# Arrays of a two-layer kernel placed at other byte addresses in SBUF

## The reference, cut to what matters

```python
nx = layer_norm(x); weights = softmax(nx @ Wq @ (ctx @ Wk).T / 16); evidence = weights @ (ctx @ Wv)
combined = concat([nx, evidence, cond])
h = silu(combined @ e_w1 + e_b1)              # 3 experts, 512 each
routed = sum((h @ e_w2 + e_b2) * softmax(combined @ router_W + router_b))
g = sigmoid(silu(combined @ gate_w1 + gate_b1) @ gate_w2 + gate_b2)
x = x + g * (routed @ out_w + out_b)
xq, xkv = ada_ln(x, cond), ada_ln(ctx, cond)
x = x + softmax(heads(xq @ Wq) @ heads(xkv @ Wk).T / 4) @ heads(xkv @ Wv) @ Wp
```

## Time and profile before

| | us |
|---|---|
| median of 3 runs (428.57, 431.21, 814.35) | 431.21 |
| the profiled execution | 429.68 |
| its span in the trace | 427.9 |
| TensorE busy with matmuls, of the span | 416.2 |
| VectorE busy | 327.5 |
| ScalarE busy | 225.6 |
| GpSimd busy | 171.2 |

### The profile page before, as it was taken

One profiled execution on the slowest core, in us unless ns is written; L12 is line 12 of the kernel. 1 busy time (PEld: TensorE's weight loads), 2 busy tenths in 40 slices (PEclk: granted clock), 3 DMA queues, 4 the chain that ended last, 5 costly groups with the idle time before them and its releaser, 6 DMA issues.

```text
span 427.9 us, 9498 instructions
## 1 busy us (share of the span) xinstructions
PE 416.2 (97%) x3541; PEld 382.9 (89%) x3541; DVE 327.5 (77%) x780; ACT 225.6 (53%) x495; POOL 171.2 (40%) x183
## 2 busy tenths in 40 slices
PE   6999989999999999999999999999999999999997
PEld 5787889899999889998999899989998998887866
DVE  1697686783876579859985799789849987994897
ACT  1887822516445644476348643862683358337272
POOL 1348484724622263225611725165315435332110
PEclk9999998999999999999999999999999999999999
DMA  8747440421300220032201300130003001410401
GB/s 293 233 157 276 173 147 2 92 57 45 70 1 5 63 64 6 23 100 51 72 7 51 75 1 2 55 75 2 3 14 88 2 4 32 106 26 2 100 2 49
DMA packets 16981, 28.06 MB, mean 66 GB/s; under 512 B 3816, under 2 KB 9128, under 8 KB 16936
## 3 DMA queue, kind: packets, MB, share of 16 engines
q1 hardware_dynamic: 16808, 27.45, 22.2%
q10 hardware_dynamic: 128, 0.01, 0.0%
HBM read 16.20 MB, written 2.10 MB: 43 GB/s over the span
## 4 chain that ended last, share of the span: by engine, by line
PE 87%; DVE 6%; ACT 4%; issue 2%; DMA 1%; DVEq 0%; ACTq 0%
PE hidden_banks L1658 9%; PE hidden_banks L1659 9%; PE hidden_banks L1660 9%; PE token_bank L1658 6%; PE token_bank L1659 6%; PE token_bank L1660 6%; PE score_banks L1665 5%; PE score_banks L2027 5%; PE score_banks L1997 4%; PE value_bank L2050 3%; PE hidden_banks L1878 3%; PE value_bank L2053 3%; PE value_bank L1665 3%; PE head_bank L1665 2%; PE value_bank L2061 1%
## 5 line engine op out<-in xcount | busy, mean ns | idle before, releaser
L1592 POOL TENSOR_TENSOR hidden_low<-hidden,hidden_high 128x512 fp32r<-128x512 f32 x56 | 72.9, 1302 | 139.3 <-ACT hidden_high L1023 139.2
L1015 ACT ACTIVATE hidden<-hidden_banks 128x512 f32<-128x512 f32 x56 | 33.3, 599 | 64.2 <-PE hidden_banks L1878 64.1
L1658 PE MATMUL hidden_banks<-normed_high,hidden_w_high 128*128 128x256 f32 x224 | 66.1, 295 | 0.8 <-DVE hidden L1348 0.8
L1431 DVE TENSOR_REDUCE head_maxima<-score_banks 128x2 f32<-128x308 f32 x128 | 56.5, 473 | 11.0 <-PE score_banks L1997 9.3
L1083 ACT ACTIVATE exp_ring<-score_banks 128x512 f32<-128x512 f32 x96 | 53.3, 604 | 21.0 <-PE score_banks L2027 17.6
L1659 PE MATMUL hidden_banks<-normed_high,hidden_w_low 128*128 128x256 f32 x224 | 63.3, 283 | 0.0
L1660 PE MATMUL hidden_banks<-normed_low,hidden_w_high 128*128 128x256 f32 x224 | 63.3, 283 | 0.0
L1658 PE MATMUL token_bank<-expert_out_high,hidden_high 128*128 128x256 f32 x192 | 55.2, 288 | 0.5 <-DVE expert_sum L1385 0.5
L1659 PE MATMUL token_bank<-expert_out_high,hidden_low 128*128 128x256 f32 x192 | 54.3, 283 | 0.0
L1660 PE MATMUL token_bank<-expert_out_low,hidden_high 128*128 128x256 f32 x192 | 54.1, 282 | 0.0
L1023 ACT CAST hidden_high<-hidden 128x512 fp32r<-128x512 f32 x56 | 34.7, 619 | 24.2 <-PE token_bank L1660 13.4
(11 more groups left out here) (288 smaller groups left out, 1133.5 us busy)
## 6 DMA issues: line engine op xcount, KB each, us to landing
unit_weights<-units SPq DMA_DIRECT2D x7, 768.0 KB, 5.2
query_stack<-queries_high SPq DMA_DIRECT2D x56, 64.0 KB, 2.0
tokens<-x SPq DMA_DIRECT2D x8, 256.0 KB, 4.8
query_stack<-queries_low SPq DMA_DIRECT2D x28, 64.0 KB, 2.0
w_slice<-units SPq DMA_DIRECT2D x7, 256.0 KB, 2.8
out<-tokens SPq DMA_DIRECT2D x7, 256.0 KB, 2.2
w_T<-folds SPq DMA_DIRECT2D x6, 256.0 KB, 4.9
pair_keys<-keys_high SPq DMA_DIRECT2D x16, 77.0 KB
```

Source lines behind the costliest of these rows:

```text
L1015: nc.scalar.activation(TB[:, ring(t, u), :], Z[:, hidden_bank(t, u), :], ACT.Tanh, scale=0.5).then_inc(scalar_z, 1)
L1431: v.tensor_reduce(MX[:, s, first:first + step + 1:step], S[:, ring_of[key][0], 0:2 * CTX].rearrange("p (j n) -> p j n", j=2), AX.X, ALU.ma ...
L1592: nc.gpsimd.tensor_tensor(SL[:, ring(t, u), :], TB[:, ring(t, u), :], raw(SH[:, ring(t, u), :]), ALU.subtract).then_inc(gpsimd_h, 1)
L1658: mm(out_, lh, rh, start=start, stop=False, skip_group_check=skip)
```

## The change

`begin(phase)` moves the running offset up to the next byte that is `phase` modulo 256. The second weights and the gate's come first, at phase 0; the first weights follow from phase 64 on, with `WQh`, `WQl`, `WPh`, `WPl` behind them in the same run; the normalized tokens and the probabilities come at phase 0, the hidden values at phase 64; `R1` starts at phase 64. Three small arrays move ahead of all of these. No instruction is added, taken away or put elsewhere, and the arrays that are laid over others go with them.

```diff
+LINE = 256
+STREAMED = 64
...
+        def begin(phase):
+            at[0] += (phase - at[0]) % LINE
+            return at[0]
...
-        weights_at = at[0]
+        COT = put("condition_silu", [P, KC, BATCH])
+        BQ = put("query_bias", [P, KC, BATCH])
+        HALF = put("minus_half", [P, NSUB])
+        experts_at = begin(0)
+        W2h = put("expert_out_high", [P, 2 * (NU - 1), D], F32R)
+        W2l = put("expert_out_low", [P, 2 * (NU - 1), D], F32R)
+        GWh = put("gate_out_high", [P, KC, D], F32R)
+        GWl = put("gate_out_low", [P, KC, D], F32R)
+        weights_at = begin(STREAMED)
         WNh = put("hidden_w_high", [P, KC, ZCOLS], F32R)
...
-        hidden_at = at[0]
+        begin(0)
+        NXh = put("normed_high", [P, 2, KC, TILE], F32R)
+        NXl = put("normed_low", [P, 2, KC, TILE], F32R)
+        PTh = put("probs_T_high", [P, 2, TILE], F32R)
+        PTl = put("probs_T_low", [P, 2, TILE], F32R)
+        PTD = put("probs_T_tail", [P, 2, TILE], F32R)
+        hidden_at = begin(STREAMED)
         TB = put("hidden", [P, 2, 512])
...
         SH = put("hidden_high", [P, 2, 512], F32R)
         SL = put("hidden_low", [P, 2, 512], F32R)
-        NXh = put("normed_high", [P, 2, KC, TILE], F32R)
-        NXl = put("normed_low", [P, 2, KC, TILE], F32R)
-        PTh = put("probs_T_high", [P, 2, TILE], F32R)
-        PTl = put("probs_T_low", [P, 2, TILE], F32R)
-        PTD = put("probs_T_tail", [P, 2, TILE], F32R)
...
-        R1 = at[0]
+        R1 = begin(STREAMED)
```

More of the change, by code:

```diff
@@ L436, in build @@
         VWD = put("context_w_tail", [BROWS, BATCH, ZCOLS], F32R)
[L437 to L441, removed]
         WQh = put("query_w_high", [P, KC, D], F32R)
@@ L456, in build @@
         B2G = put("second_bias_columns", [P, KC, P])
-        COT = put("condition_silu", [P, KC, BATCH])
         MOD = put("modulation", [P, 8, BATCH])
-        BQ = put("query_bias", [P, KC, BATCH])
-        HALF = put("minus_half", [P, NSUB])
         ST0 = put("stats0", [P, NSUB, 6])
```

## The result

| | before | changed |
|---|---|---|
| median, us | 429.89 | 423.98 |
| lowest and highest of the runs, us | 427.8 to 431.21 (one of 814.35) | 422.06 to 424.89 |
| the profiled execution's span, us | 427.9 | 423.1 |

The ratio is 0.9867, with a 95% interval of 0.9829 to 0.9905: 1.3% less time, clear of no change and less than the 2% that the prediction names. The median before counts the run of 814.35 us, the ratio does not. In a later set of runs on another occasion the changed kernel had 424.69 us against 430.01, ratio 0.9865 (0.9836 to 0.9894).

The account below looks back on a forecast made before the run. TensorE's matmul pace was taken as the bound: 8.65 us less work, 87% let through for 7.5, less 0.4 given back, net 7.1 us from 429.7, giving 422.6 us. The 8-in-10 range was 413.5 to 430.5 us.

Parts of the forecast that it names:

- the 2% that the prediction names: Whole kernel: the smallest change a measurement can tell from none, 8.6 us; faster meant under 421.1 us.
- The bound: Whole kernel: TensorE busy 416.2 of 427.9 us, 87% of the chain, clock full throughout at 2.4 GHz.
- The mechanism: za, z, p: load and stream at the same place interfere a little; a difference of 64 either way removes part.
- The pace: Long stretches of za, z, p: 120 to 115 ns a start, over 1,730 matmuls 8.65 us less TensorE work.
- the two short steps of the earlier trace: Query (difference +64) at 118.2 and 113.6 ns, proj (192) at 116.4 ns a start, before the change.
- What reaches the end: Whole kernel: 87% of TensorE's saved work, its share of the chain, shortens the time: 7.5 us.
- rival 1: za, z, p: the place hardly matters, no saving, 429.7 us, or 428 with 1 ns left; chance 0.22.
- Given back: Query and proj: difference becomes 0, costing together 0.4 us if both go to 120 ns.
- the rule that the prediction set against the change: TensorE: independent SBUF read ports for streaming and weight loads, so relative place is worth nothing; 429.7 us.
- Rival 2: za, z, p: both operands at multiples of 64 free the stream, 109.5 ns a start, 414.3 us; chance 0.22.
- Rival 3: za, z, p: difference 192 settles at a bad pace; at 123 ns a start, 434.6 us; chance 0.06.
- The 0.13 us behind the tail: Start of most behind the tail of z, 32 places: worst shown for difference 192, 122 to 130 ns.

Follow-up runs that it names:

- the six kernels of the table: Changed kernel with moving minus stationary address (modulo 256) at 0, -32, -64, -96, 128, +64: 428.42, 426.44, 423.98, 426.17, 428.87, 426.93 us.

## Why the prediction held, point by point

- **The bound.** TensorE's pace was the bound: its busy time fell by 5.1 us, no other engine's changed by more than 0.4, and the span fell by 4.8. Its clock was not full throughout, as the prediction reads it: the 8 in the earlier trace rows stands for 3.4 us of the setup at 1.2 GHz, behind 3.45 us in which TensorE was busy for 2.2. The window, with the columns of the earlier trace rows:

```profile
63.75:67.17 3.42, 3.42 (x14) 3.06 (x13) 1.43 (x8) 1.50 (x6) 0.00 (x0) 0.50 0.03 5
```

The changed kernel's profile has the same 3.4 us, so this is no part of the difference.
- **The mechanism.** Right in what it took from the rows: the place of the moving operand against the loaded one sets the pace, minus 64 is better than 0, and the name `STREAMED` marks the loaded side. That the name suggests plus 64 and the code makes minus 64, I had only noted, and I took 64 either way to be worth something; the runs put 3 us between the two (426.93 against 423.98).
- **The pace.** I took 115 ns from the two short steps of the earlier trace rows. The long stretch has 115.1, and that is luck in part: the 113.6 of the earlier trace rows is of plus 64 and of one tile in eight (the other seven have 117.6 to 118.4 in that step), and long stretches at plus 64 run at 118. The term was 120 less 115 for all 1,730, and the settled 120 is not the average before: with its entries it was 119.5, and the average after, with entries, tails and stretches in the slow pace, 115.9. So the term was 5.0 ns and should have been 3.6: 6.06 us of work saved where I had 8.65. The step that failed is this one, in its size: I set a settled pace against a settled pace, and before the change 60% of the gaps counted are of 120 ns, in the changed kernel 51% of 113 or 114.
- **What reaches the end.** I let through 87%. Of 6.06 us, 4.8 (spans) to 5.9 (medians) came through, 79 to 97%; the runs can't tell more closely. In all 7.1 us were forecast and 4.8 to 5.9 measured, and what is missing is the pace's share. The range, 413.5 to 430.5 us, holds rival 1's 429.7 as well, so that the time alone would have told little; the starts tell the two apart.
- **Given back.** Query and proj by 0.30 us, where I had 0.4; their averages went from 117.4 and 116.9 ns to 119.1 and 118.1 (so proj did not go to 120), and their loads to 190 and 189.
- **Rival 1**, that the place hardly matters, is refuted by the kernel with difference 0 against the one moved by 32: 428.42 and 422.86 us. With it falls the 429.7 us of the rule that the prediction set against the change. The Trainium skill, "SBUF — State Buffer", section "Who interferes with whom", says that only the port pair shared by VectorE and GpSimd causes contention. In this kernel's traces TensorE's starts differ by 3.6 ns in 119.5 with nothing changed but addresses, and by that rule the six kernels of the table would all have one time.
- **Rival 2**, the free stream at multiples of 64, did not come: no start of za, z or p in the changed kernel comes less than 113 ns ahead of the next, and multiples of 64 change nothing.
- **Rival 3**, a bad pace at minus 64, exists in small: 117.7 ns is the slower of its two settled paces, still better than 120. The 0.13 us behind the tail was not its price: over the 32 such places the step took 122.7 ns on average before and 117.9 in the changed kernel, at the same 192, and 114.4 with tails of 128 rows.

What stays open is why minus 64 and no other. The runs show the pace for six differences; they don't show what in the two reads meets, and I have no measurement of it. Nor do they show that it is the next matmul's stationary operand that counts and not the matmul's own: in za, z and p of every kernel here both have the same phase.

## What to carry to other kernels

Where TensorE is the bound and each matmul has its own weight load, read the pace from start to start in long stretches and hold it against the columns at the granted clock: if something is left over, the addresses of the two operands are one thing that moves it. Try the moving operand 64 bytes below the stationary one modulo 256 (here, with 256 columns against 128x128, 3.6 ns of 119.5 on average, 1.3% of the time), and measure the sign. When an effect is read from short steps, average over all that is in the stretch, entries and odd sizes too, and count the places where it applies, before the two are multiplied.

## What the hardware showed that I had not expected

- **Two settled paces at one difference.** At minus 64, 113.3 and 117.7 ns; a stretch can keep the one that it falls into, the slow one for up to 48 starts in the kernel without tails of 100 rows. Plus 64 has the same two and sits mostly in the slow one. Tails push the opposite ways, where the stretch is long enough to tell: at plus 64 they were followed by the slow pace in 6 of 6 cases in which they came in the fast one, and never ended the slow one (34 cases); at minus 64 they ended the slow one in 2 of 4 and never the fast one (36). In the changed kernel this stretch of p stays in the slow one, 22 steps from 170.54 us on, 2.59 us, 117.7 ns each:

```profile
170.54 0.28 PE L1666 MATMUL token_bank<-expert_out_high,hidden_low 128*128 128x256 f32 x1
...
173.13 0.28 PE L1667 MATMUL token_bank<-expert_out_low,hidden_high 128*128 128x256 f32 x1
```

- **What comes ahead counts.** Of the stretches of at least nine starts of za, z and p in the changed kernel, those behind a matmul of score fell into the fast pace 18 times of 20, those behind one of most 35 of 46, those that begin behind an idle wait inside these steps 17 of 32. The profile of the later set has 18, 34 and 17 of as many.
- **At 0 there is one settled pace**: 120 ns, start for start, once the entry is over; the entry can take most of a stretch (22 starts from 207.93 us in the kernel before go 124, 118, 117, 121, 120 and again to their end). At minus 32, minus 96 and 128 the longest stretch settles at none.
- **A matmul of 100 rows in the place of 128** at minus 64 in the fast pace makes the four starts behind it late, 19 to 20 ns together. At 0 the starts behind it stay at 120 ns.
